# Layer norm's root moved from ScalarE to VectorE, and its variance from one product of 512 columns to four of 128

## What is computed

```python
def layernorm(x, g, b):
    mu = jnp.mean(x, axis=-1, keepdims=True)
    var = jnp.mean(jnp.square(x - mu), axis=-1, keepdims=True)
    return (x - mu) * jax.lax.rsqrt(var + EPS) * g + b
xn = layernorm(x, norm_g, norm_b)
m = mask[..., None]
left = xn @ Wl.T * m * jax.nn.sigmoid(xn @ Wlg.T)
right = xn @ Wr.T * m * jax.nn.sigmoid(xn @ Wrg.T)
out_gate = jax.nn.sigmoid(xn @ Wog.T)
out = jnp.einsum('bikd,bjkd->bijd', left, right)
out = layernorm(out, out_norm_g, out_norm_b) * out_gate
return out @ Wout.T
```

## Time and profile before

| | |
|---|---|
| median of three runs | 2094.15 us |
| range of the runs | 2093.59 to 2095.32 us |
| the profiled execution's own time | 2098.47 us |
| its span in the trace | 2096.6 us |
| TensorE busy | 1779.0 us (85%) |
| ScalarE busy | 1372.8 us (65%) |
| VectorE busy | 1326.5 us (63%) |
| GpSimd busy | 1006.1 us (48%) |
| TensorE clock granted, mean | 0.958 of full |

### The profile page before, as it was taken

How to read it: one execution, slowest core, us unless ns; L and a number is a source line. 1 busy time by engine, 2 the same in 40 slices (tenths; PEclk the granted TensorE clock), 3 DMA queues, 4 the chain that set the end, 5 groups by cost and what they waited for, 6 DMA issues and landing times. The chain is left out here.

```text
span 2096.6 us, 40996 instructions
## 1 busy us (share of the span) xinstructions
PE 1779.0 (85%) x10389; PEld 1041.3 (50%) x10389; DVE 1326.5 (63%) x2984; ACT 1372.8 (65%) x2541; POOL 1006.1 (48%) x916
## 2 busy tenths in 40 slices
PE   0899997797998899995599799789799999699776
PEld 0445454685554445453255477633344444588433
DVE  7566666124763677776977388466377778344675
ACT  0577876355996788874499666477577787344554
POOL 0267678003991577776699300089222223000599
PEclk9999999798999999998899899999899999899999
DMA  7357876774996355546399666089547777845599
GB/s 325 123 181 235 246 231 218 268 290 170 366 367 232 101 188 173 187 149 253 135 349 366 242 217 209 32 316 375 193 150 232 234 236 216 296 179 222 187 397 377
DMA packets 326949, 496.17 MB, mean 237 GB/s; under 512 B 22828, under 2 KB 188463, under 8 KB 320439
## 3 DMA queue, kind: packets, MB, share of 16 engines
q1 hardware_dynamic: 326838, 494.93, 68.4%
HBM read 285.12 MB, written 197.13 MB: 230 GB/s over the span
## 5 line engine op out<-in xcount | busy, mean ns | idle before, releaser
L804 POOL TENSOR_TENSOR lo<-xn,hi 128x512 f16<-128x512 f32 x192 | 224.0, 1167 | 374.1 <-DVE hi L736 230.6
L601 PE MATMUL ps<-w_heads,hi 64*128 64x256 f16 x3072 | 294.0, 274 | 10.2 <-DVE sig L750 4.5
L1112 ACT ACTIVATE O<-ps 128x512 f32 (+1 forms) x144 | 151.8, 1054 | 190.5 <-PE ps L1033 190.5
L750 DVE SCALAR_TENSOR_TENSOR sig<-ps,largest,sig 128x512 f32<-128x512 f32 x256 | 180.8, 746 | 142.8 <-ACT sig L664 141.9
L664 ACT ACTIVATE sig<-ps,largest 128x512 f32<-128x512 f32 x384 | 246.2, 692 | 30.7 <-PE ps L601 28.6
L645 ACT ACTIVATE zs<-ps,shift 128x512 f32<-128x512 f32 x192 | 131.9, 687 | 191.4 <-PE ps L569 188.5
L1349 POOL TENSOR_TENSOR shared<-O,out_rs 128x128 f32<-128x128 f32 (+1 forms) x112 | 76.4, 684 | 370.8 <-DVE out_rs L1249 369.8
L601 PEld LDWEIGHTS ps<-w_heads,hi 64*128 64x128 f16 x3072 | 153.9, 95 | 167.1 <-DVE sig L750 67.3
L1397 PEld LDWEIGHTS ps<-ident,shared 128*128 128x128 f32 (+1 forms) x1024 | 120.0, 133 | 225.5 <-issue 96.4
L1397 PE MATMUL ps<-ident,shared 128*128 128x128 f32 (+1 forms) x1024 | 160.8, 282 | 75.6 <-POOL shared L1349 48.9
L601 PE MATMUL ps<-w_heads,lo 64*128 64x256 f16 x1536 | 213.5, 273 | 0.0
(11 more groups left out here) (164 smaller groups left out, 3724.3 us busy)
## 6 DMA issues: line engine op xcount, KB each, us to landing
shared<-left_right SPq DMA_DIRECT2D x34, 2048.0 KB, 12.0
shared<-gate SPq DMA_DIRECT2D x224, 256.0 KB, 4.6
gate<-gates SPq DMA_DIRECT2D x96, 512.0 KB, 2.9
x_dram<-shared SPq DMA_DIRECT2D x192, 256.0 KB, 4.3
shared<-x_dram SPq DMA_DIRECT2D x192, 256.0 KB, 4.7
xs<-x_dram SPq DMA_DIRECT2D x64, 512.0 KB, 4.2
left_right<-stage SPq DMA_DIRECT2D x64, 448.0 KB, 6.0
left_right<-shared SPq DMA_DIRECT2D x64, 448.0 KB, 5.7
```

Source lines behind the costliest of these rows:

```text
L601: last = pe.matmul(PAIR[row][:, g, kb * S:kb * S + S], tokens[half, q % 8, at:at + P], k["w_heads"][half, part, :], start=(step == 0), sto ...
L750: dve.scalar_tensor_tensor(dst, pair(row, 1), k["largest"][:, 1:2], factor, ALU.mult, ALU.mult).then_inc(pair_read.sem, 1)
L804: pool.tensor_tensor(lo[:, q % 8, :], xn[:, q % 2, :], hi[:, q % 8, :], ALU.subtract).then_inc(c["lo_done"].sem, 1)
L1112: act.activation(o_of(ch), ps[h % 4 // 2][:, h % 2, :].rearrange("p (b g i) -> p b g i", b=2, g=2), ACT.Copy).then_inc(c["o_copied"].sem, 1)
```

## The change

- **Variance.** A block's squares are multiplied in four products of 128 columns, one for each quarter of the columns, with 32 columns of `var_w` instead of 128. Quarter n of the tokens goes to partitions 32n to 32n+31 of VAR, which is now 128 rows by 128 columns. TensorE does this for four blocks together (16 products), in every fourth step, between `center` and `heads`. `sq` has four buffers instead of two.
- **Root.** VectorE makes it: VAR + EPS, a first guess by integer arithmetic on the float's bits, three Newton steps of three instructions each, then the three bf16 terms. `guess_root` and the first Newton step stand after the products of step 8k+2, the other two Newton steps between `xn` and the products of step 8k+3, `split_r` after the products of step 8k+3. All of these are 128x128. ScalarE's logarithm, exponential and their table loads are gone.
- **Move.** The terms now lie at the wrong partitions. SyncE moves them by 12 DMAs of 16 x 128 bf16 (4 KB) per batch, `move_r`, in step 8k+4 ahead of that step's load of x; `spread` of the batch's first block, in step 8k+6, waits for the last of them.
- **Leads.** Loads are 16 blocks ahead and centring 14, two more than before; `hi` and `lo` have four buffers instead of eight.

```diff
-    LOAD, CENTER, VARIANCE, SPLIT, NORM = 14, 12, 11, 3, 2
+    LOAD, CENTER, VARIANCE, GUESS, REFINE, MOVE, NORM = 16, 14, 13, 6, 5, 4, 2
+    R_STEPS, MOVES = 13, 3 * CH // P
...
+        xs, zs, sq = sb("xs", [P, 8, CH]), sb("zs", [P, 16, CH]), sb("sq", [P, GROUP, CH])
+        var, r, part = sb("var", [P, P]), sb("r", [P, P]), sb("part", [P, P])
+        terms = sb("terms", [P, 3, P], BF16)
         r_terms = sb("r_terms", [P, 2, CH], BF16)
-        xn, hi, lo = sb("xn", [P, 2, CH]), sb("hi", [P, 8, CH], F16), sb("lo", [P, 8, CH], F16)
+        xn, hi, lo = sb("xn", [P, 2, CH]), sb("hi", [P, 4, CH], F16), sb("lo", [P, 4, CH], F16)
...
-        Z, VAR, R, GATE = ps[0][:, 0, :], ps[0][:, 1, :], ps[1][:, 0, :], ps[1][:, 1, :]
+        Z, VAR, R, GATE = ps[0][:, 0, :], ps[0][:, 1, 0:P], ps[1][:, 0, :], ps[1][:, 1, :]
...
+            def move_r(i, b):
+                batch = i * (BODY // BATCH) + b
+                moved = c[f"r_moved{b % 2}"]
+                sp.wait_ge(c["r_split"].sem, c["r_split"](batch + 1))
+                sp.wait_ge(c["spread_done"].sem, c["spread_done"](batch * BATCH - BATCH))
+                for term in range(3):
+                    for quad in range(CH // P):
+                        sp.dma_start(r_terms[R_PART * term:R_PART * term + 2 * BATCH, b % 2, quad * P:quad * P + P],
+                                     terms[quad * QUAD:quad * QUAD + 2 * BATCH, term, :]).then_inc(moved.sem, 16)
             def step(i, q, more, first=False):
+                if more(MOVE) and (q + MOVE) % BATCH == 0:
+                    move_r(i, (q + MOVE) // BATCH)
                 if q % 2 == 0 and more(LOAD):
                     load(i, q + LOAD)
...
                 load(0, q)
+            move_r(0, 0)
...
-            def variance(i, q):
-                m = i * BODY + q
-                pe.wait_ge(c["sq_done"].sem, c["sq_done"](m + 1))
-                at = q % BATCH
-                if at == 0:
-                    batch = i * (BODY // BATCH) + q // BATCH
-                    pe.wait_ge(c["log_done"].sem, c["log_done"](batch))
-                w = k["var_w"][:, 2 * (BATCH - 1 - at):2 * (BATCH - 1 - at) + P]
-                pe.matmul(VAR, w, sq[:, q % 2, :], start=(at == 0), stop=(at == BATCH - 1)).then_inc(c["var_done"].sem, 1)
+            def variance(i, group):
+                for at in range(group * GROUP, group * GROUP + GROUP):
+                    m = i * BODY + at
+                    pe.wait_ge(c["sq_done"].sem, c["sq_done"](m + 1))
+                    if at % BATCH == 0:
+                        pe.wait_ge(c["var_read"].sem, c["var_read"](i * (BODY // BATCH) + at // BATCH))
+                    first = 2 * (BATCH - 1 - at % BATCH)
+                    for quad in range(CH // P):
+                        last = pe.matmul(VAR[quad * QUAD:quad * QUAD + QUAD, :], k["var_w"][:, first:first + QUAD],
+                                         sq[:, at % GROUP, quad * P:quad * P + P], start=(at % BATCH == 0), stop=(at % BATCH == BATCH - 1))
+                last.then_inc(c["var_done"].sem, 1)
...
-                pe.wait_ge(c["r_split"].sem, c["r_split"](i * (BODY // BATCH) + b + 1))
+                moved = c[f"r_moved{b % 2}"]
+                pe.wait_ge(moved.sem, moved((i * (BODY // BATCH // 2) + b // 2 + 1) * MOVES * 16))
                 pe.wait_ge(c["xn_done"].sem, c["xn_done"](m))
                 pe.matmul(R, k["spread"][:, q % BATCH, :], r_terms[:, b % 2, :], start=True, stop=True).then_inc(c["spread_done"].sem, 1)
...
                 if more(CENTER):
                     center(i, q + CENTER, Z, i * BODY + q + CENTER)
+                if more(VARIANCE) and (q + CENTER) % GROUP == 0:
+                    variance(i, (q + CENTER) // GROUP - 1)
                 heads(i, q, 0)
                 heads(i, q, 1)
                 out_gate(i, q)
-                if more(VARIANCE):
-                    variance(i, q + VARIANCE)
...
-                if q > 0:
-                    variance(0, q - 1)
+                if q > 0 and q % GROUP == 0:
+                    variance(0, q // GROUP - 1)
...
-                act.wait_ge(c["var_done"].sem, c["var_done"](m - 1))
-                act.activation(sq[:, q % 2, :], bank, ACT.Square, bias=k["shift"][:]).then_inc(c["sq_done"].sem, 1)
-            def root(i, b):
-                batch = i * (BODY // BATCH) + b
-                act.preload_act_table_set(LN_SET)
-                act.wait_ge(c["var_done"].sem, c["var_done"](batch * BATCH + BATCH))
-                act.activation(log_var[:], VAR[0:2 * BATCH, :], ACT.Ln, bias=k["unit"][0:2 * BATCH, 2:3]).then_inc(c["log_done"].sem, 1)
-                act.wait_ge(c["log_done"].sem, c["log_done"](batch + 1))
-                act.wait_ge(c["r_split"].sem, c["r_split"](batch))
-                act.activation(r[:], log_var[:], ACT.Exp, scale=-0.5).then_inc(c["r_done"].sem, 1)
+                act.wait_ge(c["var_done"].sem, c["var_done"](i * (BODY // GROUP) + q // GROUP))
+                act.activation(sq[:, q % GROUP, :], bank, ACT.Square, bias=k["shift"][:]).then_inc(c["sq_done"].sem, 1)
...
-                root_step(i, q, more)
...
+            step_of = c["r_step"]
+            def refine(count):
+                dve.tensor_tensor(part[:], r[:], r[:], ALU.mult).then_inc(step_of.sem, 1)
+                dve.wait_ge(step_of.sem, step_of(count + 1))
+                dve.scalar_tensor_tensor(part[:], part[:], -0.5, var[:], ALU.mult, ALU.mult).then_inc(step_of.sem, 1)
+                dve.wait_ge(step_of.sem, step_of(count + 2))
+                dve.scalar_tensor_tensor(r[:], part[:], 1.5, r[:], ALU.add, ALU.mult).then_inc(step_of.sem, 1)
+                dve.wait_ge(step_of.sem, step_of(count + 3))
+            def guess_root(i, b):
+                batch = i * (BODY // BATCH) + b
+                dve.wait_ge(c["var_done"].sem, c["var_done"](batch * (BATCH // GROUP) + BATCH // GROUP))
+                dve.tensor_scalar(var[:], VAR, EPS, None, ALU.add).then_inc(c["var_read"].sem, 1)
+                dve.wait_ge(c["var_read"].sem, c["var_read"](batch + 1))
+                dve.tensor_scalar(r[:].bitcast(I32), var[:].bitcast(I32), -0.5, ROOT_GUESS, ALU.mult, ALU.add).then_inc(step_of.sem, 1)
+                dve.wait_ge(step_of.sem, step_of(batch * R_STEPS + 1))
+                refine(batch * R_STEPS + 1)
+            def refine_root(i, b):
+                batch = i * (BODY // BATCH) + b
+                refine(batch * R_STEPS + 4)
+                refine(batch * R_STEPS + 7)
             def split_r(i, b):
                 batch = i * (BODY // BATCH) + b
-                parts, split = c["r_part"], c["r_split"]
-                terms = [r_terms[R_PART * part:R_PART * part + 2 * BATCH, b % 2, :] for part in range(3)]
-                dve.wait_ge(c["r_done"].sem, c["r_done"](batch + 1))
-                dve.wait_ge(c["spread_done"].sem, c["spread_done"](batch * BATCH - BATCH))
-                dve.tensor_copy(terms[0], r[:]).then_inc(parts.sem, 1)
-                dve.wait_ge(parts.sem, parts(batch * 3 + 1))
-                dve.tensor_tensor(r_rest[:], r[:], terms[0], ALU.subtract).then_inc(parts.sem, 1)
-                dve.wait_ge(parts.sem, parts(batch * 3 + 2))
-                dve.tensor_copy(r_mid[:], r_rest[:]).then_inc(parts.sem, 1)
-                dve.wait_ge(parts.sem, parts(batch * 3 + 3))
-                dve.tensor_copy(terms[1], r_mid[:])
-                dve.tensor_tensor(terms[2], r_rest[:], r_mid[:], ALU.subtract).then_inc(split.sem, 1)
-                dve.wait_ge(split.sem, split(batch + 1))
+                moved = c[f"r_moved{(b - 1) % 2}"]
+                before = i * (BODY // BATCH // 2) + (b - 1) // 2 + 1
+                dve.wait_ge(moved.sem, moved(before * MOVES * 16))
+                count = batch * R_STEPS + 10
+                dve.tensor_copy(terms[:, 0, :], r[:]).then_inc(step_of.sem, 1)
+                dve.wait_ge(step_of.sem, step_of(count + 1))
+                dve.tensor_tensor(part[:], r[:], terms[:, 0, :], ALU.subtract).then_inc(step_of.sem, 1)
+                dve.wait_ge(step_of.sem, step_of(count + 2))
+                dve.tensor_copy(terms[:, 1, :], part[:]).then_inc(step_of.sem, 1)
+                dve.wait_ge(step_of.sem, step_of(count + 3))
+                dve.tensor_tensor(terms[:, 2, :], part[:], terms[:, 1, :], ALU.subtract).then_inc(c["r_split"].sem, 1)
+                dve.wait_ge(c["r_split"].sem, c["r_split"](batch + 1))
...
                 if masked:
-                    dve.wait_ge(c["gate_mm_done"].sem, c["gate_mm_done"](m - 7))
-                    dve.tensor_tensor(hi[:, q % 8, :], zs[:, q % 16, :], R, ALU.mult).then_inc(c["hi_done"].sem, 1)
+                    dve.wait_ge(c["gate_mm_done"].sem, c["gate_mm_done"](m - 3))
+                    dve.tensor_tensor(hi[:, q % 4, :], zs[:, q % 16, :], R, ALU.mult).then_inc(c["hi_done"].sem, 1)
...
                 if more(NORM):
                     norm(i, q + NORM)
```

(10 more changed lines are left out.)

60 lines of the change are left out of this document (25 added, 35 removed).

## The result

The changed kernel takes 2302.56 us (median of 4 runs, 2300.59 to 2304.74), the kernel before 2093.87 in the same comparison: a ratio of 1.1003, 95% interval 1.0989 to 1.1017, or +208.7 us. The prediction said 2170 (+76 on the median) with a range to 2250. The sign was right, the size was not.

What follows compares the result with a forecast made beforehand. The prediction took TensorE as the bound. Full-path batches 43, last batches 1, layer starts 15, GpSimd stretching 8 and clock 8 gave +75 on 2098.5 us, the profiled execution; forecast 2170 us, range 2065 to 2250.

Steps and rivals of the forecast that it cites:

- SyncE, added: SyncE's queue: twelve small issues 0.40 us apart, 4.8 us per batch, with the load of x behind them.
- VectorE, added: VectorE: fifteen 128x128 instructions per batch at 0.33 us replace five of 16x512; `r_split` 5.2 us into step 8k+4.
- rival with VectorE shut out: VectorE's three chains each wait out a GpSimd instruction: +66 us, 2236 us; chance 11%.
- TensorE, removed and added: TensorE: 0.86 us leave each step, bursts of 1.9 us come; 5.0 us less per batch if nothing is late.
- rival that the four products don't run side by side: TensorE's variance products cost 0.86 to 1.56 us per block; at 1.2, +5.8 us per batch, 2274 us; chance 10%.
- rival that small issues are cheap: SyncE's issues cost 0.1 us, not 0.40: about 2076 us, or 2050 with VectorE at 0.2; chance 24%.
- The load, not the move, is what ends last: Before `center` of step 8k+6: the load of x lands at 22.5 us, the moved terms at 20.6.
- Two costs that come with waiting: VectorE instructions stretched by GpSimd in half of 18 batches, 8 us; TensorE's lower clock in one of three, 8 us.
- The start of each layer: Before each layer's first `spread`: instructions, issues and landing stand unhidden, +5.0 us three times, 15 us.
- last batch of each layer: End of each layer: no load stands behind the move; 1 us over all layers.
- The shorter ring of `hi` and `lo`: VectorE's `hi` of block q+2 waits for the gate of q-2, already passed by TensorE; cost put at nothing.

Runs made afterwards that it cites:

- chain_in_psum: Changed kernel with `r` and the rest of the split in PSUM, so no chain instruction has two SBUF inputs: 2264.4 us, ratio 1.0821.
- load_first: Changed kernel with SyncE's load of x put ahead of the twelve moves, nothing else changed: 2242.95 us, ratio 1.0724.
- warm: Changed kernel with overwritten filler products on TensorE ahead of the two waits of step 8k+6: 2257.18 us, ratio 1.0785.
- best: Changed kernel without moves (TensorE spreads two fp16 terms from the quarters), VectorE's chain in smaller lots, `r` in PSUM: 2056.36 us.
- best_one_table: best plus one line: ScalarE loads the table set holding the sigmoid at its loop body's head: 2039.12 us, ratio 0.9736.

## Why the prediction was wrong in size

The path was the predicted one, from VectorE's chain over the issues and the load to `center`; the terms on it were too small. Two failed together: "SyncE, added" (54 us over the 18 regular batches) and "VectorE, added" (46 us, of which 8 had been put down for GpSimd). The third is the clock. The rival with VectorE shut out (2236) kept the sum's issues and clock, and so stays below 2302.

- **"TensorE, removed and added" held.** A step without the variance is 3.25 us, and the burst of four blocks is 1.08 us at full clock, under the 1.9 I took; the rival that the four products don't run side by side is refuted. By the Trainium skill's factor (TensorE: Matmul & The Clock Gate, the table of Part 3) I had estimated 0.36 us per block, from three tiles of 512 columns; the trace has 0.27. All variance products of the program (ns, min/median/max):
```profile
L597 PE MATMUL ps<-sq,var_w x1536: 272/273/423, 70.0 to 1946.0; 128*32 128x128 f32 x192
```
  A record is 273 ns long, and 32 of them end in 1.08 us: they overlap.
- **"VectorE, added": the first step on the path that failed.** "The nearest row is ... 0.33 us to the next start" is right for an instruction alone (0.29 to 0.33), but the chain's sum left GpSimd out. I had it as a rival at 11% for 66 us, because most of the 24 instructions of the earlier trace rows were not stretched. Those stand at another place of the step, and such a row says how often *that* place meets GpSimd. By the groups' means (mean less the shortest, times the count, over the batches) the lock lengthens the chain 3.0 us per batch in layer 0, 4.4 in layer 1 and 0.8 in layer 3; chain_in_psum gave 38 us back, net of PSUM's longer access and of SyncE's stores in layer 0. The 8 us that I had put down for it are the mis-sized term.
- **"SyncE, added": mis-sized.** "Two tiny DMAs start 0.40 us apart; twelve are 4.8 us, and I take that whatever the size." Those rows were two loads of constants; the moves within SBUF have a median of 0.59 (ns, min/median/max):
```profile
L543 SPq DMA_DIRECT2D r_terms<-terms x276: 512/589/1622, 119.3 to 1965.1; - x138
```
  The twelve are 7.5 us (786.30 to 793.77), +2.7 in this batch; over the 18 batches they take 7.5 to 8.5 us. The rival that small issues are cheap, my way to "faster" with 24%, is refuted from the other side.
- **"The load, not the move, is what ends last" held**, for 59.6 us (load_first); the landing of the moves is 1.7 us, under the 2.2 assumed.
- **"Two costs that come with waiting": the clock was mis-sized.** I took 1.3 us in one batch in three, 8 us. Over the regular batches of layer 1 the changed kernel's mean clock (third number from the end) is 0.84, and much the same in layers 0 and 3 (0.87 and 0.86):
```profile
774.40:1004.90 230.50, 167.57 (x1501) 87.10 (x1520) 146.84 (x237) 131.70 (x204) 127.45 (x80) 0.84 0.41 132
```
  and the fall behind the two waits of step 8k+6 alone is worth 2.0 us per regular batch, and 45 us in all (warm).
- **"The start of each layer"** was +5.0; in layer 0 the first spread's weights now load at 90.6 us instead of 86.8, +3.8. From the cast that fills `spread` to that load it is 14.7, 14.8 and 15.7 us in the three layers instead of 7.7; in layer 0 the cast itself comes 3.2 us earlier. The starts and the last batch of each layer, together 16 us in my sum, are among the 38 us that lie outside the regular batches.
- **A part I did not see**: with the root gone, the table loads beside it go, but two of 1.28 us now stand at the head of ScalarE's loop body, nine pairs in the changed kernel as in best, where the step took 5.6 us instead of 3.5 (best_one_table).

What stays open: how the 38 us outside the regular batches divide between the starts, the last batches and the rest; and the clock behind VectorE's hold-up at 780 to 787, which was not tested by itself. The shorter ring of `hi` and `lo`, which I had put at nothing, was not undone in any run either. In layer 1 of the changed kernel VectorE's `hi` waits for the gate's products once, for 0.2 us; as far as that shows, the ring cost next to nothing.
